# A decoder block on one core: the scores' place behind a pair's values, engine orders laid out anew, and four slices of a layer norm scaled on ScalarE

## The chip, the cores and the metric

One Trainium2 chip, of which the kernel uses one core. The metric is the device time of one execution in microseconds (us). A core has TensorE (matrix products, called PE in the profile), VectorE (DVE), ScalarE (ACT) and GpSimd (POOL), and SyncE (SP), whose instructions here are all DMA transfers. Each engine carries out its own list of instructions in order. The engines wait for one another by semaphores. TensorE writes into eight PSUM banks of 128 x 512 float32.

## The reference

Layer norm, cross attention with causal mask (32 query heads, 8 key and value heads), a gate and a residual; then layer norm, a gated feed-forward part with scaled weights, a gate and a residual. All in float32; x has 32 x 64 rows of 512.

```python
Q = (q @ Wq.T).reshape(b, s, HKV, exp, DK)      # q = layernorm(x), exp = 4, DK = 128
K = (k @ Wk.T).reshape(b, s, HKV, DK)           # k = v = ctx_4096
V = (v @ Wv.T).reshape(b, s, HKV, DV)
scores = jnp.einsum('bqhed,bkhd->bheqk', Q, K) * scale
scores = jnp.where(causal, scores, jnp.finfo(scores.dtype).min)
probs = jax.nn.softmax(scores, axis=-1)
attn = jnp.einsum('bheqk,bkhd->bqhed', probs, V).reshape(b, s, H * DV)
...
x = x + jnp.tanh(g_xattn[0]) * (attn @ Wd.T)
x = x + jnp.tanh(g_ffn[0]) * ffn(layernorm(x))  # silu(a) * b, then the down product
```

## The kernel before

Every large product is made of three products of rounded parts: a float32 operand is split into a high part (a rounded copy, made by ScalarE) and a low part (operand less high part, made by VectorE or GpSimd), and high x high, high x low and low x high are summed.

The program has three stages. In the first, 44 "quads" (0 to about 500 us) make values, keys and queries and write them to DRAM. The second is attention, from 500 to 985 us. The third is the feed-forward part, 28 blocks from 985 us to the end. The change is in the second stage and its borders.

Attention has NU = 64 units (a key head and 256 rows of x), which are taken in pairs: a step p of the loop `for p in range(2, NPAIR)` (NPAIR = 32) works with u = 2p. A unit passes through these functions, each on the engine named; "b" is one of two halves:

- `scores(u)` (PE): q times k into bank 6 (even u) or 7 (odd u).
- `turned(u)` (DVE): a transpose out of the bank into `prob`; `masked(u)` (POOL) adds the mask; `maxima(u)` (DVE) makes `own_max`; once per pair `other_maxima(p)` (ACT) moves the maxima across partitions, and `row_maxima(p)` (DVE) joins them.
- `less_max(u)` (POOL) subtracts, `exponentials(u)` (ACT), `sums(u)` (DVE) makes `own_sum`, `other_sums(p)` (ACT) moves, `inverse(p)` (DVE) makes `row_inv`, `over_sum(u)` (POOL) multiplies, `probs_turned(u)` (DVE) transposes into `pt`.
- `weighted_values(u)` (PE) makes pt times v into banks 4 and 5 (even u) or 2 and 3 (odd u); `out_hi(u)` (ACT) and `out_lo(u)` (DVE) split that into `o_hi[u % 2]` and `o_lo`.
- `output(i)`, i = 2u and 2u + 1 (PE): twelve matmuls with the split weights `wd_hi` and `wd_lo` into one bank; `add_to_x(i)` (DVE) multiplies by the gate and adds to X in SBUF.

The lines on which the order of these depends are waits on buffers. ScalarE's out_hi may overwrite o_hi only when the outputs of the unit two before are complete:

```python
        def out_hi(u):
            a.wait_ge(p_o, u + 1)
            if u >= 2:
                a.wait_ge(p_y, 2 * u - 2)
```

`p_y` counts outputs, `p_o` values, `v_y` additions to X, `v_turn` the transposes out of the score banks, `v_o` and `a_o` halves of out_lo and out_hi, `g_wd` low halves of wd. An output with t == 0 waits for out_lo of its unit and for its key head's four low halves of wd (`g_wd`, `output_lo` on POOL; the high halves, `output_hi`, on ACT); two of the four are made per step, the last two of head k in step 2k + 1. The outputs share banks 0 and 1, and every fourth one uses bank 6.

The second layer norm's slices 0 to 3 (two tiles of 128 rows each) are made ready inside the loop: in step 18 + 3m the statistics (`stats2`, `ln_moments` on DVE; `ln_pow`, and `apply2` for the scaling, on POOL), in the next step the transposes (`columns2` on PE) and their copies out of banks 2 and 3 (`x2_columns` on ACT, awaited by `weighted_values(u - 1)` through `a_xt2`) with `x2_sums` on POOL, and in the step after it the split (`x2_hi_of` on ACT, `x2_lo_of` on DVE, which waits for it). Step 30 holds POOL's and ACT's work for the first gate and up weights (`ffn_left_sums`, `ffn_left_lo`, `gate_up_hi`).

All orders are written out by hand, engine by engine.

## Time and profile before

| | |
|---|---|
| time, median of 3 runs | 1430.93 us (1430.73 to 1432.84) |
| the profiled execution: time, span | 1430.72 us, 1428.7 us |
| busy: PE, PEld, DVE | 1400.6, 1125.3, 1016.2 us |
| busy: ACT, POOL | 640.3, 1038.6 us |
| DMA traffic | 217.96 MB, mean 153 GB/s |

The span is what the profiler sees from the first to the last instruction; 2.0 us of the time lie outside it. PE is the matmul side of TensorE, PEld its loading of weights, which overlaps. An engine's busy time is what its instructions took, so its waits are the rest.

### The profile page before, as it was taken

The numbers are of one execution on the slowest core, as the hardware profiler recorded it, in microseconds if no ns is written. First come the engines' busy times: TensorE is split into PE (matmuls) and PEld (weight loads), VectorE is DVE, ScalarE is ACT, GpSimd is POOL, SyncE is SP. The second block draws the span as 40 slices with busy tenths as digits, with TensorE's granted clock in tenths as the row PEclk, the third lists the DMA queues.
The fourth block names the chain that finished last, engine by engine and source line by source line (L and its number), as shares of the span: only waits on it lengthen the run. The fifth ranks groups of instructions, "written<-read, shape, count | busy, mean of one in ns | idle before, by whom it ended". The sixth has DMA issues, their size and how long they took to land.

```text
span 1428.7 us, 19944 instructions
## 1 busy us (share of the span) xinstructions
PE 1400.6 (98%) x6810; PEld 1125.3 (79%) x6810; DVE 1016.2 (71%) x1549; ACT 640.3 (45%) x1246; POOL 1038.6 (73%) x919
## 2 busy tenths in 40 slices
PE   8999999999999999999999999999999999999998
PEld 8988788888887767777776766767888888888887
DVE  6487777777465677777776776775688878676776
ACT  6465555554444344443443444444344434343433
POOL 5599999998879556656656777775678886666664
PEclk9999999999999999999999999999999999999999
DMA  8477787778887745434443433331112112212112
GB/s 282 150 251 226 233 270 257 253 254 282 307 264 264 254 156 199 140 125 142 135 152 118 155 116 120 127 132 31 45 45 60 52 45 65 105 47 65 45 59 74
DMA packets 116067, 217.96 MB, mean 153 GB/s; under 512 B 9472, under 2 KB 47616, under 8 KB 113920
## 3 DMA queue, kind: packets, MB, share of 16 engines
q1 hardware_dynamic: 115968, 216.70, 46.1%
q8 instruction: 55, 0.90, 0.3%
q14 instruction: 44, 0.36, 0.1%
HBM read 151.13 MB, written 65.54 MB: 152 GB/s over the span
## 4 chain that ended last, share of the span: by engine, by line
PE 82%; POOL 8%; DVE 4%; issue 3%; ACT 1%; DMA 1%; SPq 0%; DVEq 0%; POOLq 0%; ACTq 0%
PE bank L574 65%; PE bank L848 3%; PE bank L849 3%; PE bank L850 3%; PE bank L697 3%; PE bank L722 3%; POOL prob L1663 2%; POOL xn L1677 1%; POOL wd_lo L1649 1%; POOL prob L1657 1%; POOL prob L1669 1%; DVE X L1386 1%; POOL wa_lo L1643 1%; PE bank L621 1%; DMA q_sb<-q_scratch 0%
## 5 line engine op out<-in xcount | busy, mean ns | idle before, releaser
L574 PE MATMUL bank<-xc,wa_hi 128*128 128x512 f32 x896 | 277.4, 391 | 0.0
L574 PE MATMUL bank<-wd_hi,o_hi 128*128 128x512 f32 x512 | 207.9, 406 | 5.0 <-issue 3.5
L574 PE MATMUL bank<-wd_lo,o_hi 128*128 128x512 f32 x512 | 200.8, 392 | 0.0
L574 PE MATMUL bank<-wd_hi,o_lo 128*128 128x512 f32 x512 | 199.5, 390 | 0.0
L574 PEld LDWEIGHTS bank<-xc,wa_hi 128*128 128x128 f32 x896 | 167.7, 188 | 36.4 <-issue 1.1
L574 PE MATMUL bank<-xc,wa_lo 128*128 128x512 f32 x448 | 174.5, 390 | 0.0
L1455 DVE SCALAR_TENSOR_TENSOR X<-bank,tg,X 128x512 f32<-128x512 f32 x221 | 154.5, 742 | 0.0
L574 PE MATMUL bank<-x_hi,wf_hi 128*128 128x512 f32 x392 | 153.0, 390 | 0.0
L574 PE MATMUL bank<-x_hi,wf_lo 128*128 128x512 f32 x392 | 152.6, 389 | 0.0
L574 PE MATMUL bank<-x_lo,wf_hi 128*128 128x512 f32 x364 | 141.7, 389 | 0.0
L1669 POOL TENSOR_TENSOR prob<-prob,row_inv 128x512 f32<-128x512 f32 x64 | 72.5, 1153 | 94.6 <-DVE row_inv L1356 94.6
L1386 DVE SCALAR_TENSOR_TENSOR X<-bank,tg,X 128x512 f32<-128x512 f32 x128 | 94.7, 741 | 65.2 <-PE bank L574 65.2
L574 PEld LDWEIGHTS bank<-wd_hi,o_hi 128*128 128x128 f32 x512 | 96.1, 188 | 47.9 <-issue 27.7
L574 PEld LDWEIGHTS bank<-wd_hi,o_lo 128*128 128x128 f32 x512 | 96.3, 188 | 21.3
L574 PEld LDWEIGHTS bank<-wd_lo,o_hi 128*128 128x128 f32 x512 | 96.3, 188 | 17.7
L1022 ACT ACTIVATE other_max<-own_max 32x32 f32<-32x32 f32 x128 | 29.1, 227 | 178.8 <-DVE own_max L1338 176.4
L1657 POOL TENSOR_TENSOR prob<-prob,mask 128x512 f32<-128x512 f32 x64 | 81.2, 1290 | 34.5 <-DVE prob L1334 34.5
L1300 DVE TENSOR_TENSOR t<-bank,s 128x512 f32<-128x512 f32 x44 | 30.3, 689 | 99.9 <-PE bank L574 99.7
L1375 DVE TENSOR_TENSOR o_lo<-bank,o_hi 128x512 fp32r<-128x512 f32 x128 | 82.1, 684 | 23.4 <-ACT o_hi L1042 23.4
L574 PEld LDWEIGHTS bank<-xc,wa_lo 128*128 128x128 f32 x448 | 84.1, 188 | 17.9
L1643 POOL TENSOR_TENSOR wa_lo<-w_raw,wa_hi 128x512 fp32r<-128x512 f32 x72 | 76.5, 1084 | 24.8 <-ACT wa_hi L951 24.7
L1643 POOL TENSOR_TENSOR wa_lo<-ws,wa_hi 128x1024 fp32r<-128x1024 f32 x36 | 92.5, 2570 | 0.0
(181 smaller groups left out, 3424.7 us busy)
## 6 DMA issues: line engine op xcount, KB each, us to landing
q_scratch<-q_st SPq DMA_DIRECT2D x32, 1024.0 KB, 4.4
q_sb<-q_scratch SPq DMA_DIRECT2D x64, 512.0 KB, 4.9
w_raw<-in_wq SPq DMA_DIRECT2D x32, 512.0 KB, 4.4
wd_raw<-in_wd SPq DMA_DIRECT2D x16, 1024.0 KB, 5.1
f_raw<-ffn_eff_scratch SPq DMA_DIRECT2D x28, 512.0 KB, 3.6
er_raw<-in_sf_r SPq DMA_DIRECT2D x42, 256.0 KB, 3.9
e_raw<-in_wf SPq DMA_DIRECT2D x42, 256.0 KB, 5.4
ffn_eff_scratch<-e_eff SPq DMA_DIRECT2D x42, 256.0 KB, 5.2
```

The costliest lines, as they stand in the source:

```text
L574: last = pe.matmul(to, a, b, start=(start and n == 0), stop=(stop and n == 3 * len(pairs) - 1), skip_group_check=onto)
L697: last = pe.matmul(bank[score_bank(u)][b * S:(b + 1) * S, t * 256:(t + 1) * 256], k_sb[u % 2][:, cb * S:(cb + 1) * S], q_sb[u % 2][:, :, c ...
L722: last = pe.matmul(bank[value_bank(u) + b][:, t * 256:(t + 1) * 256], v_sb[u % 2][rows, t, :], pt_of(u)[rows, t, :], start=True, stop=True)
L848: pe.matmul(to, d_hi[b][:, half, cols], dn_hi[n == NF - 1][:, :], start=True, stop=False)
L849: pe.matmul(to, d_hi[b][:, half, cols], dn_lo[n == NF - 1][:, :], start=False, stop=False)
L850: pe.matmul(to, d_lo[b][:, half, cols], dn_hi[n == NF - 1][:, :], start=False, stop=True).then_inc(p_yf, 1)
L1375: v.tensor_tensor(lo, bank[value_bank(u) + b][:, :].rearrange("p (t e s) -> p t e s", t=CT, e=G), f32(hi), ALU.subtract).then_inc(v_o, 1)
L1386: v.scalar_tensor_tensor(to, bank[output_bank(i)][:, :], tg[:, 0:1], to, ALU.mult, ALU.add).then_inc(v_y, 1)
L1455: v.scalar_tensor_tensor(to, bank[down_bank(n, k)][:, :], tg[:, 1:2], to, ALU.mult, ALU.add).then_inc(v_yf, 1)
L1643: g.tensor_tensor(wa_lo[p][:, part, :, :].rearrange("p n k d -> p (n k d)"), raw, f32(wa_hi[p][:, part, :, :]).rearrange("p n k d -> p (n ...
L1657: g.tensor_tensor(to, to, mask[:, :].rearrange("p (o k) -> p o k", o=1).broadcast_to([P, NR // 2, S]), ALU.add).then_inc(g_mask, 1)
L1669: g.tensor_tensor(to, to, row_inv[:, u % 2, :].rearrange("p (n o) -> p n o", o=1).broadcast_to([P, NR, HS]), ALU.mult).then_inc(g_p, 1)
```

## The change

The work is the same except for one thing: the scaling of slices 0 to 3 of the second layer norm, (x - mean) x rstd on GpSimd, becomes x x rstd + shift on ScalarE, with shift = -mean x rstd made by two small operations more. Everything else is order, and which bank an output uses (bank 6 goes from i % 4 == 3 to i % 4 == 1), so that waits on banks change with it.

On TensorE `scores(u + 2)` and `scores(u + 3)` stand directly behind the two `weighted_values`, where they stood two outputs later. SyncE loads q and k a pair earlier. On the other engines the step is written out anew. The core of the diff:

```diff
@@ PE: waits of scores and outputs
             if u >= 6 and u % 2 == 0:
-                pe.wait_ge(v_y, 2 * u - 8)
+                pe.wait_ge(v_y, 2 * u - 10)
...
-            elif i < 2 * NU - 4 and i % 4 == 3:
-
-                pe.wait_ge(v_turn, min(2 * ((i + 5) // 4), NU - 2) + 1)
+            elif i < 2 * NU - 4 and i % 4 == 1:
+
+                pe.wait_ge(v_turn, min((i + 7) // 2, NU - 2) + 1)
+            elif i == 2 * NU - 5:
+                pe.wait_ge(v_y, i - 1)
@@ PE: order
+        output(0)
         weighted_values(1)
-        output(0)
+        scores(4)
+        scores(5)
         for p in range(2, NPAIR):
             u = 2 * p
-            scores(u)
-            scores(u + 1)
             output(2 * u - 7)
...
             output(2 * u - 6)
             weighted_values(u - 2)
             weighted_values(u - 1)
+            if p + 1 < NPAIR:
+                scores(u + 2)
+                scores(u + 3)
             output(2 * u - 5)
             output(2 * u - 4)
@@ ACT
+        def apply2(m):
+            a.wait_ge(g_nm, 8 + m + 1)
+            if m:
+                a.wait_ge(p_xt2, 2 * m)
+            for p in range(2):
+                a.activation(xn2[:, p, :], X[:, 2 * m + p, :], ACT.Identity, bias=shift[:, p:p + 1],
+                             scale=rstd[:, p:p + 1]).then_inc(a_xn2, 1)
...
         for p in range(2, NPAIR):
             u = 2 * p
+            exponentials(u)
+            exponentials(u + 1)
+            other_sums(p)
             if p in WD_STEP:
                 k, heads = WD_STEP[p]
                 for e in heads:
                     output_hi(k, e)
             if p in COLUMNS1:
                 x2_columns(COLUMNS1[p], (2, 3))
-            other_maxima(p)
             out_hi(u - 2)
-            exponentials(u)
-            exponentials(u + 1)
+            out_hi(u - 1)
             if p in SPLIT1:
                 x2_hi_of(SPLIT1[p])
-            other_sums(p)
+            if p in ROWS1:
+                apply2(ROWS1[p])
+            if p + 1 < NPAIR:
+                other_maxima(p + 1)
             if p == F_FIRST:
                 for part in range(3):
                     gate_up_hi(0, part)
-            out_hi(u - 1)
@@ DVE: quad(NQ - 1), behind its second sum
+            if q == NQ - 1:
+                maxima(2)
+                maxima(3)
+                v.wait_ge(a_tanh, 1)
+                out_lo(0)
@@ DVE: the step
             add_to_x(2 * u - 8)
-            out_lo(u - 3)
-            turned(u)
-            turned(u + 1)
-            probs_turned(u - 2)
-            probs_turned(u - 1)
-            add_to_x(2 * u - 7)
-            maxima(u)
-            maxima(u + 1)
-            add_to_x(2 * u - 6)
-            row_maxima(p)
-            out_lo(u - 2)
             sums(u)
             sums(u + 1)
-            add_to_x(2 * u - 5)
+            add_to_x(2 * u - 7)
             inverse(p)
-            if p in SPLIT1:
-                x2_lo_of(SPLIT1[p])
             if p in ROWS1:
                 stats2(ROWS1[p])
                 ln_moments(8 + ROWS1[p])
+            if p in SPLIT1:
+                x2_lo_of(SPLIT1[p])
+            add_to_x(2 * u - 6)
+            out_lo(u - 2)
+            if p + 1 < NPAIR:
+                turned(u + 2)
+                turned(u + 3)
+            out_lo(u - 1)
+            probs_turned(u)
+            probs_turned(u + 1)
+            add_to_x(2 * u - 5)
+            if p + 1 < NPAIR:
+                maxima(u + 2)
+                maxima(u + 3)
+                row_maxima(p + 1)
@@ POOL: the step
-            over_sum(u - 2)
-            over_sum(u - 1)
-            masked(u)
-            masked(u + 1)
-            if p in COLUMNS1:
-                x2_sums(COLUMNS1[p])
+            over_sum(u)
+            over_sum(u + 1)
             if p in WD_STEP:
                 k, heads = WD_STEP[p]
                 for e in heads:
                     output_lo(k, e)
-            less_max(u)
-            less_max(u + 1)
             if p in ROWS1:
                 ln_pow(8 + ROWS1[p])
-                apply2(ROWS1[p])
+            if p + 1 < NPAIR:
+                masked(u + 2)
+                masked(u + 3)
+                less_max(u + 2)
+                less_max(u + 3)
+            if p in COLUMNS1:
+                x2_sums(COLUMNS1[p])
```

VectorE in step 20, the first split step, from `inverse(20)` on. Before (X_124 is X, o_lo1 with o_hi1 is unit 37, whose values are one step old, prob2 and prob3 are the buffers, in a ring of four, into which the next pair's scores are turned):

```order
L1356 RECIPROCAL row_inv_67<-row_sum_66 128x32
L1410 TENSOR_TENSOR x2_lo0_154<-xb2_151,x2_hi0_152 128x1792
L1386 SCALAR_TENSOR_TENSOR X_124<-bank1,tg_52,X_124 128x512
L1375 TENSOR_TENSOR o_lo1_147<-bank2,o_hi1_145 128x2x4x64
L1375 TENSOR_TENSOR o_lo1_147<-bank3,o_hi1_145 128x2x4x64
L1334 STREAM_TRANSPOSE prob2_136<-bank6 128x512
```

The same place after the change:

```order
L1386 RECIPROCAL row_inv_67<-row_sum_66 128x32
L1443 TENSOR_TENSOR x2_lo0_154<-xb2_151,x2_hi0_152 128x1792
L1416 SCALAR_TENSOR_TENSOR X_124<-bank1,tg_52,X_124 128x512
L1405 TENSOR_TENSOR o_lo0_146<-bank4,o_hi0_144 128x2x4x64
L1405 TENSOR_TENSOR o_lo0_146<-bank5,o_hi0_144 128x2x4x64
L1364 STREAM_TRANSPOSE prob2_136<-bank6 128x512
L1364 STREAM_TRANSPOSE prob3_137<-bank7 128x512
L1405 TENSOR_TENSOR o_lo1_147<-bank2,o_hi1_145 128x2x4x64
```

The low part x2_lo0 stands behind the reciprocal both times; what follows it is now out_lo of both units of this step's values, with the transposes between them.

ScalarE in step 20. Before:

```order
L1022 ACTIVATE other_max_62<-own_max_61 32x32 x4
L1042 ACTIVATE o_hi0_144<-bank4 128x2x4x64
L1042 ACTIVATE o_hi0_144<-bank5 128x2x4x64
L1035 ACTIVATE prob0_134<-prob0_134 128x512
L1035 ACTIVATE prob1_135<-prob1_135 128x512
L1068 ACTIVATE x2_hi0_152<-xb2_151 128x1792
L1030 ACTIVATE other_sum_65<-own_sum_64 32x32 x4
L1042 ACTIVATE o_hi1_145<-bank2 128x2x4x64
```

After:

```order
L1043 ACTIVATE other_sum_65<-own_sum_64 32x32 x4
L1028 ACTIVATE wd_hi0_126<-wd_raw_125 128x512 x2
L1055 ACTIVATE o_hi0_144<-bank4 128x2x4x64
L1055 ACTIVATE o_hi0_144<-bank5 128x2x4x64
L1055 ACTIVATE o_hi1_145<-bank2 128x2x4x64
L1055 ACTIVATE o_hi1_145<-bank3 128x2x4x64
L1089 ACTIVATE x2_hi0_152<-xb2_151 128x1792
L1035 ACTIVATE other_max_62<-own_max_61 32x32 x4
```

The high part x2_hi0, for which VectorE's x2_lo0 waits, has moved from ahead of the moved sums and of o_hi1 to behind both.

GpSimd where steps 30 and 31 meet (fs and wf are the first gate and up weights). Before:

```order
L1649 TENSOR_TENSOR wd_lo1_129<-wd_raw_125,wd_hi1_127 128x512 x2
L1663 TENSOR_TENSOR prob0_134<-prob0_134,row_max_63 128x512
L1663 TENSOR_TENSOR prob1_135<-prob1_135,row_max_63 128x512
L1699 TENSOR_TENSOR fs_160<-f_raw_159 128x256
...
L1710 TENSOR_TENSOR wf_lo_158<-fs_160,wf_hi_157 128x1024
L1669 TENSOR_TENSOR prob0_134<-prob0_134,row_inv_67 128x512
L1669 TENSOR_TENSOR prob1_135<-prob1_135,row_inv_67 128x512
L1657 TENSOR_TENSOR prob2_136<-prob2_136,mask_51 128x512
L1657 TENSOR_TENSOR prob3_137<-prob3_137,mask_51 128x512
L1649 TENSOR_TENSOR wd_lo1_129<-wd_raw_125,wd_hi1_127 128x512 x2
L1663 TENSOR_TENSOR prob2_136<-prob2_136,row_max_63 128x512
```

After:

```order
L1701 TENSOR_TENSOR prob2_136<-prob2_136,row_max_63 128x512
L1701 TENSOR_TENSOR prob3_137<-prob3_137,row_max_63 128x512
L1737 TENSOR_TENSOR fs_160<-f_raw_159 128x256
...
L1748 TENSOR_TENSOR wf_lo_158<-fs_160,wf_hi_157 128x1024
L1707 TENSOR_TENSOR prob2_136<-prob2_136,row_inv_67 128x512
L1707 TENSOR_TENSOR prob3_137<-prob3_137,row_inv_67 128x512
L1687 TENSOR_TENSOR wd_lo1_129<-wd_raw_125,wd_hi1_127 128x512 x2
```

The last two low halves of wd stood ahead of the last pair's subtraction of the maxima (prob2, prob3 with row_max); now they stand behind it, behind the weights' seven operations and behind that pair's multiplication with row_inv.

## Rows read from the trace of the kernel before

**Rows 1.** The page's busy time of one engine: us, share of span, instructions

```profile
PE 1400.6 (98%) x6810; PEld 1125.3 (79%) x6810; DVE 1016.2 (71%) x1549; ACT 640.3 (45%) x1246; POOL 1038.6 (73%) x919
```

**Rows 2.** Timeline of a plain step: start us, length us, engine, line, out<-in [idle before <-releaser]

```profile
673.76 1.95 PE L697 MATMUL bank<-q_sb,k_sb 128*64 128x256 f32 x16
...
675.63 0.50 PE L574 MATMUL bank<-wd_hi,o_hi 128*128 128x512 f32 x1
...
675.97 0.40 PE L574 MATMUL bank<-wd_lo,o_hi 128*128 128x512 f32 x1
...
678.69 0.75 DVE L1386 SCALAR_TENSOR_TENSOR X<-bank,tg,X 128x512 f32<-128x512 f32 x1 [0.47 <-PE bank L574]
...
681.30 2.00 PE L722 MATMUL bank<-pt,v_sb 64*128 64x256 f32 x16
...
682.48 1.09 ACT L1042 ACTIVATE o_hi<-bank 128x512 fp32r<-128x512 f32 x2 [0.84 <-PE bank L722]
683.18 1.29 DVE L1375 TENSOR_TENSOR o_lo<-bank,o_hi 128x512 fp32r<-128x512 f32 x2 [0.92 <-ACT o_hi L1042]
...
683.22 0.50 PE L574 MATMUL bank<-wd_hi,o_hi 128*128 128x512 f32 x1
```

**Rows 3.** Timeline of the entry into the loop, 503 to 515 us

```profile
504.26 0.19 DVE L1344 TENSOR_TENSOR row_max<-own_max,other_max 128x32 f32<-128x32 f32 x1 [1.05 <-ACT other_max L1022]
...
504.53 2.06 POOL L1663 TENSOR_TENSOR prob<-prob,row_max 128x512 f32<-128x512 f32 x2 [7.67 <-DVE row_max L1344]
...
508.00 0.98 ACT L1030 ACTIVATE other_sum<-own_sum 32x32 f32<-32x32 f32 x4 [0.75 <-DVE own_sum L1348]
...
509.67 2.05 POOL L1669 TENSOR_TENSOR prob<-prob,row_inv 128x512 f32<-128x512 f32 x2 [3.09 <-DVE row_inv L1356]
...
514.39 2.00 PE L722 MATMUL bank<-pt,v_sb 64*128 64x256 f32 x16
```

**Rows 4.** Timeline of the stop behind slice 1's columns, 833 to 837 us

```profile
833.31 0.98 ACT L1030 ACTIVATE other_sum<-own_sum 32x32 f32<-32x32 f32 x4 [0.75 <-DVE own_sum L1348]
...
834.08 3.07 PE L697 MATMUL bank<-q_sb,k_sb 128*64 128x256 f32 x16 [2.75 <-DVE X L1386]
```

**Rows 5.** Timeline of the end of the loop, 960 to 975 us

```profile
961.67 0.74 POOL L1699 TENSOR_TENSOR fs<-f_raw 128x256 f32<-128x256 f32 x1
...
969.14 2.06 POOL L1669 TENSOR_TENSOR prob<-prob,row_inv 128x512 f32<-128x512 f32 x2
...
973.43 2.00 PE L722 MATMUL bank<-pt,v_sb 64*128 64x256 f32 x16
```

**Rows 6.** Timeline of VectorE's hand-overs without a wait, 785 to 792 us

```profile
785.44 1.28 DVE L1375 TENSOR_TENSOR o_lo<-bank,o_hi 128x512 fp32r<-128x512 f32 x2
...
786.64 1.30 DVE L1334 STREAM_TRANSPOSE prob<-bank 128x512 f32<-128x512 f32 x2
...
787.87 1.26 DVE L1362 STREAM_TRANSPOSE pt<-prob 128x512 f32<-128x512 f32 x2
789.09 0.75 DVE L1386 SCALAR_TENSOR_TENSOR X<-bank,tg,X 128x512 f32<-128x512 f32 x1
789.76 1.27 DVE L1338 TENSOR_REDUCE own_max<-prob 128x16 f32<-128x512 f32 x2
...
791.06 0.98 ACT L1022 ACTIVATE other_max<-own_max 32x32 f32<-32x32 f32 x4 [4.43 <-DVE own_max L1338]
```

**Rows 7.** Timelines of POOL, ACT and DVE around slice 0, 755 to 801 us

```profile
765.93 4.14 POOL L1677 TENSOR_SCALAR xn<-X,moments,rstd 128x512 f32<-128x512 f32 x2
...
777.42 2.51 POOL L1649 TENSOR_TENSOR wd_lo<-wd_raw,wd_hi 128x512 fp32r<-128x512 f32 x2
...
795.37 1.69 ACT L1068 ACTIVATE x_hi<-xb 128x1792 fp32r<-128x1792 f32 x1
...
798.59 1.96 DVE L1410 TENSOR_TENSOR x_lo<-xb,x_hi 128x1792 fp32r<-128x1792 f32 x1
```

**Rows 8.** Busy time and granted TensorE clock (PEclk) of one stretch

```profile
834.60:838.00 3.40, 3.40 (x16) 2.12 (x13) 3.40 (x7) 1.95 (x4) 2.68 (x3) 0.52 0.40 150
```

More of the change, by code:

```diff
@@ L203, in flamingo @@
     a_c0, a_chi, a_k, a_w1, a_tanh = sem("a_c0"), sem("a_chi"), sem("a_k"), sem("a_w1"), sem("a_tanh")
+    a_xn2 = sem("a_xn2")
     a_xt, a_xhi, a_wa, a_s1, a_s5, a_c11 = (sem("a_xt"), sem("a_xhi"), sem("a_wa"), sem("a_s1"), sem("a_s5"),
@@ L290, in flamingo @@
     NPAIR = NU // 2
+    SHARED = (0, None, 1, 2)
     def output_bank(i):
@@ L294, in output_bank @@
             return 4 + i - (2 * NU - 4)
-        return 6 if i % 4 == 3 else (3 * (i // 4) + i % 4) % 2
+        return 6 if i % 4 == 1 or i == 2 * NU - 5 else (3 * (i // 4) + SHARED[i % 4]) % 2
     def output_before(i):
-        n = 3 * (i // 4) + i % 4 - 2
-        return 4 * (n // 3) + n % 3
+        n = 3 * (i // 4) + SHARED[i % 4] - 2
+        return 4 * (n // 3) + SHARED.index(n % 3)
     def score_bank(u):
@@ L500, in _ @@
                 load_v(3)
+                load_q_k(6)
+                load_q_k(7)
             if q == Q0 + NHP:
@@ L532, in _ @@
             u = 2 * p
-            for n in range(u + 2, min(u + 4, NU)):
-                load_q_k(n)
             load_v(u)
             load_v(u + 1)
+            for n in range(u + 4, min(u + 6, NU)):
+                load_q_k(n)
             if p == 4:
@@ L735, in output @@
                 pe.wait_ge(a_c11, NQ)
-            elif i == 1:
+            elif i == 2:
                 pe.wait_ge(v_t2, NQ)
-            elif i < 2 * NU - 4 and i % 4 == 3:
-                pe.wait_ge(v_turn, min(2 * ((i + 5) // 4), NU - 2) + 1)
+            elif i < 2 * NU - 4 and i % 4 == 1:
+                pe.wait_ge(v_turn, min((i + 7) // 2, NU - 2) + 1)
+            elif i == 2 * NU - 5:
+                pe.wait_ge(v_y, i - 1)
             elif i < 2 * NU - 4:
@@ L748, in columns2 @@
             for p in range(2):
-                pe.wait_ge(g_xn, 2 * m + p + 1)
+                if m < 4:
+                    pe.wait_ge(a_xn2, 2 * m + p + 1)
+                else:
+                    pe.wait_ge(g_xn, 2 * (m - 4) + p + 1)
                 for k in range(KC):
@@ L1181, in _ @@
         other_maxima(1)
+        out_hi(1)
         exponentials(2)
@@ L1184, in _ @@
         other_sums(1)
-        out_hi(1)
+        other_maxima(2)
         for p in range(2, NPAIR):
             u = 2 * p
+            exponentials(u)
+            exponentials(u + 1)
+            other_sums(p)
             if p in WD_STEP:
@@ L1242, in ln_moments @@
             v.wait_ge(v_bn, 2 * n + 2)
-            if 1 <= n <= 8:
+            if 1 <= n <= 12:
                 v.wait_ge(g_nm, n)
@@ L1248, in ln_moments @@
             v.tensor_scalar(veps[:, :], moments[:, :, 1], EPS, None, ALU.add).then_inc(v_eps, 1)
-            if n < 8:
+            if n < 12:
                 v.tensor_scalar(neg_mean[:, :], moments[:, :, 0], -1.0, None, ALU.mult).then_inc(v_nm, 1)
@@ L1390, in stats2 @@
             if m:
-                v.wait_ge(g_xn, 2 * m)
+                if m <= 4:
+                    v.wait_ge(a_xn2, 2 * m)
+                else:
+                    v.wait_ge(g_xn, 2 * (m - 4))
             ln_bn(lambda p: X[:, 2 * m + p, :])
@@ L1479, in _ @@
             quad(q)
-        v.wait_ge(a_tanh, 1)
-        out_lo(0)
-        maxima(2)
-        maxima(3)
         row_maxima(1)
+        out_lo(1)
         sums(2)
         sums(3)
+        turned(4)
+        turned(5)
         inverse(1)
+        probs_turned(2)
+        probs_turned(3)
+        maxima(4)
+        maxima(5)
+        row_maxima(2)
         for p in range(2, NPAIR):
@@ L1510, in _ @@
                 ln_moments(8 + ROWS1[p])
+            if p in SPLIT1:
[13 more added lines that the diff above has]
+                row_maxima(p + 1)
         add_to_x(2 * NU - 8)
-        out_lo(NU - 3)
-        probs_turned(NU - 2)
-        probs_turned(NU - 1)
         for i in range(2 * NU - 7, 2 * NU - 4):
@@ L1599, in ln_pow @@
                 g.wait_ge(a_xn, 2 * n)
+            elif 8 < n <= 12:
+                g.wait_ge(a_xn2, 2 * (n - 8))
             g.tensor_tensor(rstd[:, :], veps[:, :], neg_half[:, :], ALU.pow).then_inc(g_pow, 1)
-            if n < 8:
+            if n < 12:
                 g.wait_ge(g_pow, n + 1)
@@ L1787, in _ @@
         less_max(3)
+        over_sum(2)
+        over_sum(3)
+        masked(4)
+        masked(5)
+        less_max(4)
+        less_max(5)
         for p in range(2, NPAIR):
             u = 2 * p
-            over_sum(u - 2)
-            over_sum(u - 1)
-            masked(u)
-            masked(u + 1)
-            if p in COLUMNS1:
-                x2_sums(COLUMNS1[p])
+            over_sum(u)
+            over_sum(u + 1)
             if p in WD_STEP:
@@ L1808, in _ @@
                     ffn_left_lo(0, part)
-        over_sum(NU - 2)
-        over_sum(NU - 1)
         for n in range(NF):
```

## The prediction

> **What bounds the kernel now.** I read the engines' busy table first: TensorE is busy for 98% of the span [rows 1], so only a stop of TensorE, or a change in what it executes, can move the time. Then I read the timeline of the stretch in which attention's pairs run, 505 to 980 us, because every edit lies there. In what follows a step p is one turn of the pair loop (u = 2p), V is the start of its pair of values on TensorE and Sc the start of its pair of scores. From V of step 2 at 514.39 to a plain V at 681.30 there are 11 steps [rows 2, 3], so a plain step takes 166.91 / 11 = 15.17 us. In it TensorE never stops: scores go from 673.76 to 675.63 (1.87), values from 681.30 to 683.22 (1.92), and the remaining 11.38 are four outputs, 2.85 each [rows 2]. VectorE and GpSimd trail behind in that step, and their order costs nothing. It does cost at the four slices of the second layer norm, where TensorE stops, for example 2.75 us ahead of the scores at 834.08, until VectorE's addition to X has emptied bank 6 [rows 4]. All of step 2 to step 31 is 973.43 - 514.39 = 459.04 us [rows 3, 5]; 29 plain steps are 439.9, so the four slices cost 19.1 us, some 4 of them the transposes themselves (32 of 128 columns, an estimate from the 512-column matmuls' 0.23), 15 stops.
>
> **What the joining of values and scores gives.** The first output matmul after scores is followed by the next after 0.34 us (675.63 to 675.97), where an output's twelve average 2.85 / 12 = 0.24 [rows 2]: changing from one kind of matmul to another costs about 0.1 going out, and I take as much going in. Scores directly behind values save the way out of one block and the way in of the next, about 0.2 per step (from 0 to 0.4). TensorE alone would then need 15.17 - 0.2 = 14.97 us a step. The 30 joinings are worth 6 us (0 to 12), provided that nothing else becomes slower than 14.97.
>
> **The plain step afterwards.** I follow what has to happen between one Sc and the next. ScalarE now stands with out_hi(u-1) right behind out_hi(u-2), and VectorE has out_lo(u-1), probs_turned, add_to_x(2u-5) and maxima(u+2) behind one another. But out_hi(u-1) overwrites the half of o_hi that output(2u-5) reads (its wait on p_y is 2u-4), and output(2u-5) stands behind the scores. So from Sc: 1.87 scores and 3.06 until the other engines see that output complete (675.63 to 678.69) [rows 2] make 4.93; o_hi to o_lo 0.70 (682.48 to 683.18) [rows 2]; o_lo 1.20, the turned probabilities 1.22, one addition 0.67, two maxima until ScalarE moves them 1.30, by the starts 785.44, 786.64, 787.87, 789.09, 789.76, 791.06 [rows 6]; the move 0.98 and 0.03 of hand-over [rows 6]; row_max to less_max 0.27 and less_max to other_sum 3.47 [rows 3]; other_sum to the released scores 0.77 (833.31 to 834.08), which holds add_to_x(2u-3) of bank 6 [rows 4]. The sum is 15.54. These are one loop: add_to_x(2u-3) must be done for scores(u+4). It is 0.57 longer than TensorE's 14.97 and 0.37 longer than the step now. In the order of before nothing closes this loop, since out_hi(u-1) stands behind the sums and is not waited for by the maxima.
>
> In odd steps GpSimd's low halves of wd are needed by output(2u-4). They start 2.02 behind over_sum, which starts 3.47 + 1.67 behind less_max (508.00 to 509.67) [rows 3], take 2.51 [rows 7], and 0.2 of hand-over follows: 9.9 from less_max, and less_max of this pair lies at Sc - 4.24. So output(2u-4) starts at Sc + 5.65 in place of 1.87 + 2.87 = Sc + 4.74; of these 0.9 us the slack of 0.57 swallows the larger part, 0.34 is left. Plain steps: 15.54 even, 15.88 odd.
>
> **The entry.** The first output now waits for out_lo(0) about as long as values(1) waited. Then over_sum(2) starts near 510.0 (509.67 now) [rows 3], with masked(4), (5) behind it: 2.02 + 2.5 (as wd_lo, the row of GpSimd that is nearest) [rows 7], the last maximum 0.7, its move 1.01, 0.27: less_max(4) at 516.6. scores(6) need add_to_x(1), so Sc of step 2 is 516.6 + 4.24 = 520.8, while values(3) end at about 516.5: a stop of 4.3 us. From Sc of step 2 to Sc of step 18 there are 16 plain steps: 8 x 15.54 + 8 x 15.88 = 251.4, that is 772.2.
>
> **The slices, three steps each.** (a) The step with the statistics, and on to the next Sc: x2_columns stand on ScalarE behind other_sums and two copies, and values(u-1) wait for them. less_max at Sc + 11.30 (15.54 - 4.24); then 3.47 + 0.98, two copies 1.1 and two more 1.1 (as the o_hi pair, 1.09 [rows 2]), hand-overs 0.3: 18.3; half the values 1.0: the next Sc at +19.3. (b) The step with the columns: 15.54. (c) The step with the split: x2_lo_of stands on VectorE ahead of add_to_x(2u-6), out_lo(u-2) and both turned, but x2_hi_of stands on ScalarE behind out_hi(u-1), which waits for output(2u-5). So Sc + 4.93, o_hi 1.06, x_hi 1.69, x_lo from 7.72 until 9.60 (1.96 less overlap) [rows 7], the addition 0.67, out_lo 1.28, hand-over 0.15: output(2u-4), wanted at 4.74, starts at 11.7, a stop of 7.0 us. Going on with turned 1.20 behind out_lo's start at 10.25, then 1.22 to out_lo(u-1) at 12.67, 1.20, 1.22, 0.67, 1.30, 1.01, 0.27 gives less_max at 18.3 and the next Sc at 22.6. The three make 57.4 in place of 3 x 15.17 + 4.8 = 50.3. Four slices: 229.6, so Sc of step 30 is 1001.8.
>
> **The way out.** In step 31 output(120) needs the last low halves of wd. They stood ahead of less_max(62); now they stand behind it, behind the seven GpSimd operations for the first gate and up weights (961.67 to 969.14, 7.47) [rows 5] and behind over_sum(62). less_max(62) at 1001.8 + 11.3 = 1013.1; 2.03 + 7.47, or by way of ScalarE, whose exponentials now wait behind the copy of those weights, 9.7; then 2.02 + 2.51 + 0.2: output(120) at 1027.6, after a stop of 8 us. Now it starts at 973.43 + 1.92 + 2.87 = 978.2 [rows 5]. Everything behind it (the last outputs, the feed-forward part) is unchanged and its inputs are early, so it shifts by 1027.6 - 978.2 = 49.4 us.
>
> **The clock.** After the stop that ends at 834.08 the granted clock was 0.52 for 3.4 us, the level of 1.2 GHz, and that pair of scores took 3.07 in place of 1.95 [rows 2, 4, 8]; such a dip costs 3.4 x 0.5 = 1.7 us on TensorE. I count it once for the entry, once for the way out, and for the four split steps 1.1 each (their 0.6 of slack covers a part): 7.8 us. The sum: 1430.7 (the profiled execution, 0.2 under the median of the runs) + 49.4 + 7.8 = 1488 us.
>
> **Moving the scaling of slices 0 to 3.** GpSimd loses 4.14 us per slice [rows 7]; ScalarE gains two activations, costed at nothing: they stand between out_hi(u-1), done at Sc + 6.0, and other_maxima, which can't start before Sc + 10.0. If that cover were gone, each would add its own time, some 0.7. The Trainium skill (GPSIMD Engine Reference, Engine selection) says that an elementwise operation with one input runs on GpSimd at roughly line rate. By that the move would free only about 1.5 us per slice; the trace has 2.07 for each of the two [rows 7], and the trace decides. The sum would be the same by either, since GpSimd is not in the loop of a plain step.
>
> **The rivals.** *Faster:* the longer way from scores to values (eight outputs in place of six) covers everything. TensorE goes at 14.97, and with 4 x 4.14 us taken from GpSimd the stops at the slices vanish: 1430.7 - 6 - 15 = 1410. It holds if the loop above is under 14.97 and x2_hi_of doesn't wait for an output. For it: GpSimd's waits and scaling are what the slices wait on now. Against it: 15.54 by rows, and the order itself. *The split does not stop TensorE:* say it finds its high half early; 4 x 7.0 and four dips less: 1455. *The loop does not bind plain steps:* hand-overs overlap better; 16 steps at about 14.97 in place of 15.71: 12 us less, and 2 at the slices: 1474. *All stops dip the clock,* the 3.3 us ones at the columns too (now the one of [rows 4] dipped, and no other): four more at 1.7, and 0.6 at each split: 1497. *It evens out:* the joinings pay for one stop: 1431.
>
> **How the numbers follow.** Forecast 0.70 (its own range 1474 to 1499, from 0 to 12 for the joinings, 0.2 either way in 27 loops, and dips from none to all); 1497 and beyond 0.05; split harmless 0.09; loop not binding 0.08; faster 0.06; even 0.02. To leave out no more than 2 in 10 the range reaches down to the harmless split: 1455 to 1500. A measurement tells about 0.2% (3 us) from no change. Faster 0.06, the same 0.02, slower 0.92.
>
> **What would show it.** In the profile after: plain steps of 15.5 to 15.9 us from V to V, with a stop of about half a microsecond ahead of scores, waiting for VectorE's addition; o_hi of the second unit right behind the third output after the values; a stop of about 4 us ahead of scores(6); four of about 7 ahead of output(2u-4) while VectorE waits for x_hi; about 3 inside the values of the columns steps; about 8 in step 31 behind wd_lo. I am wrong if plain steps run at 15.0, or if x_lo doesn't hold VectorE up.

## The result, and the profile after

The changed kernel takes 1495.78 us (median of 4 runs, 1494.75 to 1495.96), the kernel before 1431.88 on the same chip. The ratio of the two means is 1.0443 (95% interval 1.0425 to 1.0461), so it is 4.4% slower. The forecast was 1488 in a range of 1455 to 1500. The profiled execution took 1495.64 us, its span is 1493.8.

The page's busy line of the changed kernel, against [rows 1]:

```profile
PE 1412.2 (95%) x6810; PEld 1138.1 (76%) x6810; DVE 1017.3 (68%) x1553; ACT 641.5 (43%) x1254; POOL 1015.3 (68%) x915
```

TensorE executes the same 6810 matmuls, 11.6 us longer (they run at half the clock behind stops), and it is idle in 5% of the span in place of 2%. What it waited for from 520 to 1050 us, in the view of waits (us in total, times, longest):

```profile
PE bank L579 <- DVE o_lo L1405: 27.1, 4, 6.8
PE bank L727 <- ACT xb L1074: 12.8, 4, 3.2
PE bank L702 <- DVE X L1416: 9.8, 13, 2.6
PE bank L579 <- POOL wd_lo L1687: 7.8, 1, 7.8
PE bank L579 <- ACT o_hi L1055: 6.2, 8, 0.9
```

The first line is the four split steps (outputs wait for out_lo), the second the four steps with columns (values wait for x2_columns), the third the even plain steps and the four columns steps (scores wait for an addition to X) with the entry, the fourth step 31, the fifth the eight odd plain steps.

Three pairs of scores follow one another in plain steps, from TensorE's timeline:

```profile
555.19 1.95 PE L702 MATMUL bank<-q_sb,k_sb 128*64 128x256 f32 x16
...
570.77 1.95 PE L702 MATMUL bank<-q_sb,k_sb 128*64 128x256 f32 x16 [0.60 <-DVE X L1416]
...
586.68 1.95 PE L702 MATMUL bank<-q_sb,k_sb 128*64 128x256 f32 x16
```

15.58 and 15.91 us, where [rows 2] gave 15.17. The stop of the odd step, ahead of output(2u - 4):

```profile
573.69 2.52 POOL L1687 TENSOR_TENSOR wd_lo<-wd_raw,wd_hi 128x512 fp32r<-128x512 f32 x2
...
576.42 0.47 PE L579 MATMUL bank<-wd_hi,o_hi 128*128 128x512 f32 x1 [0.76 <-ACT o_hi L1055]
```

The view names ScalarE's o_hi, but the one made just then is unit u - 1's, and by its code this output waits for unit u - 2's, made 3 us earlier. Of all that it does wait for, GpSimd's wd_lo ends last.

The split step of slice 0, all engines:

```profile
815.62 1.08 ACT L1055 ACTIVATE o_hi<-bank 128x512 fp32r<-128x512 f32 x2 [2.65 <-PE bank L579]
816.60 1.70 ACT L1089 ACTIVATE x_hi<-xb 128x1792 fp32r<-128x1792 f32 x1
818.33 2.02 DVE L1443 TENSOR_TENSOR x_lo<-xb,x_hi 128x1792 fp32r<-128x1792 f32 x1 [6.59 <-ACT x_hi L1089]
820.27 0.74 DVE L1416 SCALAR_TENSOR_TENSOR X<-bank,tg,X 128x512 f32<-128x512 f32 x1
820.93 1.28 DVE L1405 TENSOR_TENSOR o_lo<-bank,o_hi 128x512 fp32r<-128x512 f32 x2
...
822.31 0.77 PE L579 MATMUL bank<-wd_hi,o_hi 128*128 128x512 f32 x1 [6.78 <-DVE o_lo L1405]
```

Read it downwards: ScalarE's o_hi of the second unit waits for an output; x_hi stands behind it; VectorE has waited 6.59 us for x_hi, and the addition and o_lo stand behind x_lo. The first matmul takes 0.77, since the clock has fallen. Here are busy times, with the granted clock after the engines, of the 4.2 us behind that stop and of the stretch behind the columns stop of slice 1:

```profile
822.30:826.50 4.20, 4.19 (x10) 3.33 (x11) 4.20 (x8) 0.00 (x0) 2.52 (x2) 0.50 0.00 0
...
852.60:857.30 4.70, 4.66 (x25) 2.49 (x25) 2.01 (x3) 0.87 (x2) 3.77 (x4) 0.64 0.22 51
```

The four stops of 6.8 us and the one of 7.8 were all followed by the level of 1.2 GHz; of the four of 3.2 us, two were (slices 1 and 3), two were not. The way out, GpSimd and ScalarE, and the output that waits:

```profile
1031.18 1.06 ACT L1108 ACTIVATE wf_hi<-fs 128x1024 fp32r<-128x1024 f32 x1 [4.29 <-POOL fs L1742]
1032.14 1.13 ACT L1048 ACTIVATE prob<-prob 128x512 f32<-128x512 f32 x2
...
1035.92 2.05 POOL L1707 TENSOR_TENSOR prob<-prob,row_inv 128x512 f32<-128x512 f32 x2 [0.51 <-DVE row_inv L1386]
...
1037.93 2.50 POOL L1687 TENSOR_TENSOR wd_lo<-wd_raw,wd_hi 128x512 fp32r<-128x512 f32 x2
1040.64 0.77 PE L579 MATMUL bank<-wd_hi,o_hi 128*128 128x512 f32 x1 [7.79 <-POOL wd_lo L1687]
```

So the account of the profiled executions is, by the start of output(120) and of the scores: 1040.64 against 978.2, 62.4 us later; 2.1 us more by the last pair's values (the clock behind that stop), 0.6 to the end: 65.1.

### The profile page after: what moved, and what is told of

Same layout as the page of the kernel before. It is cut to its first block, busy times and chain, and to the rows that moved or that the text cites. A ratio compares the mean times of both kernels' runs of the same rounds, so it can differ in the third digit from the quotient of the medians.

```text
span 1493.8 us, 19964 instructions
## 1 busy us (share of the span) xinstructions
PE 1412.2 (95%) x6810; PEld 1138.1 (76%) x6810; DVE 1017.3 (68%) x1553; ACT 641.5 (43%) x1254; POOL 1015.3 (68%) x915
## 4 chain that ended last, share of the span: by engine, by line
PE 73%; DVE 10%; POOL 6%; ACT 5%; issue 4%; DMA 2%; SPq 1%; DVEq 0%; ACTq 0%; POOLq 0%
PE bank L579 56%; PE bank L702 4%; PE bank L862 3%; PE bank L863 3%; PE bank L861 3%; POOL prob L1701 3%; PE bank L727 2%; DVE o_lo L1405 2%; DVE X L1416 2%; DVE own_max L1368 1%; ACT o_hi L1055 1%; ACT other_max L1035 1%; DVE pt L1392 1%; DVE own_sum L1378 1%; DMA er_raw<-in_sf_r 1%
## 5 line engine op out<-in xcount | busy, mean ns | idle before, releaser
L579 PE MATMUL bank<-wd_lo,o_hi 128*128 128x512 f32 x512 | 204.2, 399 | 0.0
L579 PE MATMUL bank<-wd_hi,o_lo 128*128 128x512 f32 x512 | 204.2, 399 | 0.0
L579 PEld LDWEIGHTS bank<-wd_hi,o_hi 128*128 128x128 f32 x512 | 99.2, 194 | 82.5 <-issue 50.9
L1701 POOL TENSOR_TENSOR prob<-prob,row_max 128x512 f32<-128x512 f32 x64 | 65.9, 1051 | 128.4 <-DVE row_max L1374 128.4
L1707 POOL TENSOR_TENSOR prob<-prob,row_inv 128x512 f32<-128x512 f32 x64 | 65.8, 1048 | 92.7 <-DVE row_inv L1386 92.7
L1055 ACT ACTIVATE o_hi<-bank 128x512 fp32r<-128x512 f32 x128 | 68.8, 591 | 106.2 <-PE bank L579 99.5
L579 PEld LDWEIGHTS bank<-wd_lo,o_hi 128*128 128x128 f32 x512 | 99.4, 194 | 19.6
```

The lines of the kernel that those rows point to most:

```text
L579: last = pe.matmul(to, a, b, start=(start and n == 0), stop=(stop and n == 3 * len(pairs) - 1), skip_group_check=onto)
L1055: a.activation(o_hi[u % 2][:, :, :].rearrange("p e (t b s) -> p b t e s", t=CT, b=2)[:, b], bank[value_bank(u) + b][:, :].rearrange("p (t ...
L1701: g.tensor_tensor(to, to, row_max[:, u % 2, :].rearrange("p (n o) -> p n o", o=1).broadcast_to([P, NR, HS]), ALU.subtract).then_inc(g_sub, 1)
L1707: g.tensor_tensor(to, to, row_inv[:, u % 2, :].rearrange("p (n o) -> p n o", o=1).broadcast_to([P, NR, HS]), ALU.mult).then_inc(g_p, 1)
```

## The experiments

Eleven kernels ran, all measured against the kernel before on their own chip, whose medians were 1432.1 to 1432.6. "Changed" below is the changed kernel.

**Split step.** VectorE's low half at the end of the step.

```diff
-            if p in SPLIT1:
-                x2_lo_of(SPLIT1[p])
             add_to_x(2 * u - 6)
...
                 row_maxima(p + 1)
+            if p in SPLIT1:
+                x2_lo_of(SPLIT1[p])
```

> The changed kernel with one edit: VectorE's x2_lo_of of the split steps moved to the end of the step, behind row_maxima(p + 1). My theory (VectorE waits for ScalarE's x2_hi_of, which stands behind out_hi(u - 1), and out_lo(u - 2) stands behind it): all four stops of 6.8 us ahead of output(2u - 4) and their clock dips go, a split step falls from 23.9 or 24.4 us between scores to 15.6 or 15.9, the kernel from 1496 to about 1463. Rival (what stops TensorE there is the addition or out_hi itself, and the low half only rides along): the stops stay above 4 us and the time above 1485.

Measured: 1470.44 us (1468.13 to 1473.31), ratio 1.0266 (1.0249 to 1.0282), 25 us under changed. The waits for o_lo are gone altogether, so the mechanism holds. But it is 7 us above what I expected: split steps take 17.3 to 17.6 us where I had put 15.6 or 15.9. The timeline shows why:

```profile
822.12 2.02 DVE L1443 TENSOR_TENSOR x_lo<-xb,x_hi 128x1792 fp32r<-128x1792 f32 x1
...
822.28 3.77 POOL L1701 TENSOR_TENSOR prob<-prob,row_max 128x512 f32<-128x512 f32 x2 [3.08 <-DVE row_max L1374]
```

GpSimd's pair of less_max takes 3.77 us there and 2.06 in every other step. I tested that by doing the operation twice, with the same values.

```diff
                 if blk == 0:
+                    v.tensor_tensor(to[:, s]..., xb2[:, ...]..., x2_hi[...]..., ALU.subtract).then_inc(v_twice, 1)
+                    v.wait_ge(v_twice, m + 1)
```

> The kernel with x2_lo_of at the end of the split step, whose time was 7 us above what I expected, with that operation done twice in a row, the same values both times. My theory (GpSimd's less_max starts 0.16 us behind it and makes no headway while VectorE works on x2_lo, so that the pair takes 3.77 in place of 2.06 us): the pair then takes 5.5 to 5.8, the four steps get 2 us longer each, about 1478 (1475 to 1483). Rival (the 3.77 comes from something else, and VectorE has 3 us idle there that hide a second operation): less_max stays at 3.77 and the time within 3 us of 1470.

Measured: 1481.69 us (1480.19 to 1484.57), 11 above the single one. GpSimd's pair, and VectorE's second subtraction, now take:

```profile
822.43 5.55 POOL L1708 TENSOR_TENSOR prob<-prob,row_max 128x512 f32<-128x512 f32 x2 [3.06 <-DVE row_max L1375]
...
824.32 2.75 DVE L1450 TENSOR_TENSOR x_lo<-xb,x_hi 128x1792 fp32r<-128x1792 f32 x1
```

The theory holds: GpSimd makes next to no headway while VectorE works on x_lo. It goes the other way too: the second subtraction takes 2.75 us where the first takes 2.02, with GpSimd's first operation of the pair between the two. The time is in the range that I gave, though the median rose by 11 us where I had put 8: in the profiled executions (9.5 us apart) the four split steps are 1.4 to 1.8 us longer each, the three steps behind them 0.5 to 1.3, and one columns step 1.6, by a further clock dip.

**Plain step.** The cut of the loop, and of one other term of it.

```diff
-            out_lo(u - 1)
             probs_turned(u)
             probs_turned(u + 1)
             add_to_x(2 * u - 5)
             if p + 1 < NPAIR:
                 maxima(u + 2)
                 maxima(u + 3)
+            out_lo(u - 1)
+            if p + 1 < NPAIR:
                 row_maxima(p + 1)
```

> The changed kernel with one edit: VectorE's out_lo(u - 1) moved behind probs_turned, add_to_x(2u - 5) and the two maxima, so that the maxima of the next pair no longer wait for an output that stands behind the scores. My theory (a loop of 15.5 to 15.9 us from scores to scores by way of output(2u - 5), out_hi(u - 1), out_lo(u - 1), maxima, sums, add_to_x): plain steps fall to TensorE's own 14.9 to 15.0, the stops ahead of scores and in odd steps behind wd_lo go, the columns stops shrink from 3.2 to about 1, and the time falls from 1496 to about 1468; the split stops of 6.8 us stay. Rival (the plain step is bound by GpSimd's or the scores' own hand-overs): plain steps stay at 15.5 or more and the time above 1490.

Measured: 1460.90 us (1459.86 to 1464.11), ratio 1.0202 (1.0187 to 1.0217): 35 us under changed, 7 better than expected. Every plain step is TensorE's own:

```profile
552.85 1.95 PE L702 MATMUL bank<-q_sb,k_sb 128*64 128x256 f32 x16
...
567.76 1.95 PE L702 MATMUL bank<-q_sb,k_sb 128*64 128x256 f32 x16
...
582.68 1.95 PE L702 MATMUL bank<-q_sb,k_sb 128*64 128x256 f32 x16
```

The waits that are left, 520 to 1060 us:

```profile
PE bank L579 <- DVE o_lo L1405: 31.9, 5, 6.8
PE bank L702 <- DVE X L1416: 4.3, 1, 4.3
PE bank L727 <- ACT xb L1074: 3.1, 4, 1.0
```

Thirteen waits for the addition have become one (the entry), the waits for o_hi are gone, the columns stops fell from 3.2 to 1.0 without a clock dip. In step 31 the wait for wd_lo shrank to one of 4.8 us for o_lo.

The second cut leaves out_lo(u - 1) where the change put it and takes the turned probabilities out from behind it:

```diff
             out_lo(u - 1)
-            probs_turned(u)
-            probs_turned(u + 1)
             add_to_x(2 * u - 5)
             if p + 1 < NPAIR:
                 maxima(u + 2)
                 maxima(u + 3)
+            probs_turned(u)
+            probs_turned(u + 1)
+            if p + 1 < NPAIR:
                 row_maxima(p + 1)
```

> The changed kernel with one edit: VectorE's probs_turned(u), (u + 1) (1.2 us) moved out from between out_lo(u - 1) and the maxima, to behind them; out_lo(u - 1) stays where the change put it. It asks whether the loop is a sum of terms, as my prediction had it, so that taking out any term of it shortens the step by that term until TensorE's own 14.91 is reached. By the loop: even plain steps fall from 15.58 by up to 1.2, that is to 14.91; odd ones keep 0.1 to 0.4 of stop behind the low halves of wd; the columns and split stops shrink by 1.2 each: 1472 us (1468 to 1480). Rival (only the wait for output(2u - 5) itself matters, what stands between is hidden): plain steps stay at 15.6 and 15.9, above 1490.

Measured: 1479.39 us (1477.29 to 1482.60), ratio 1.0326 (1.0308 to 1.0344). Plain steps are 14.91 and 15.49 us; outside the entry the wait for the addition is gone, and the four columns stops are 8.3 us together, from 12.8. So the loop is a sum, as forecast. That the split stops would shrink by 1.2 us too was wrong: they are 6.8 still, since the turned probabilities stand behind out_lo(u - 2) there and are no part of that stop; this is 5 of the 7 us by which I missed.

**Way out.** The last halves of the output weights in step 30, ahead of less_max(62).

```diff
@@ ACT, step 30, ahead of other_maxima(p + 1), and no longer in step 31
+            if p == NPAIR - 2:
+                for e in WD_STEP[NPAIR - 1][1]:
+                    output_hi(WD_STEP[NPAIR - 1][0], e)
@@ POOL, step 30, ahead of less_max(u + 2), and no longer in step 31
+            if p == NPAIR - 2:
+                for e in WD_STEP[NPAIR - 1][1]:
+                    output_lo(WD_STEP[NPAIR - 1][0], e)
```

> The changed kernel with one edit: the last two halves of the output weights (high on ScalarE, low on GpSimd) made one step earlier, in step 30 ahead of less_max(62) and of the first gate and up weights. My theory (output(120) waits for them behind seven operations and over_sum(62)): the stop of 7.8 us in step 31 and its clock dip go, 1496 to about 1487, all else unchanged. Rival (over_sum(62), turned or the values of the last pair are as late, and the stop only moves behind output(120)): above 1493.

Measured: 1492.65 us (1491.63 to 1494.49), ratio 1.0421 (1.0405 to 1.0437). That is 6 us above what I expected and just under what the rival had (above 1493). Neither was quite right: the stop neither went nor moved behind output(120), but stayed ahead of it, went from 7.8 to 4.9 us and changed its name.

```profile
1030.56 1.06 ACT L1108 ACTIVATE wf_hi<-fs 128x1024 fp32r<-128x1024 f32 x1 [4.30 <-POOL fs L1745]
1031.53 1.13 ACT L1048 ACTIVATE prob<-prob 128x512 f32<-128x512 f32 x2
1033.48 0.98 ACT L1043 ACTIVATE other_sum<-own_sum 32x32 f32<-32x32 f32 x4 [0.83 <-DVE own_sum L1381]
1034.49 2.06 ACT L1055 ACTIVATE o_hi<-bank 128x512 fp32r<-128x512 f32 x4
...
1037.09 0.77 PE L579 MATMUL bank<-wd_hi,o_hi 128*128 128x512 f32 x1 [4.86 <-DVE o_lo L1408]
```

ScalarE waits 4.3 us for GpSimd's sums of the first gate and up weights; exponentials(62), the sums and o_hi queue behind that copy. So I moved those weights too:

```diff
@@ ACT and POOL: in step 30
-            if p == F_FIRST:
-                ...
@@ ACT and POOL: behind the loop
+        for part in range(3):
+            gate_up_hi(0, part)
...
+        ffn_left_sums(0)
+        for part in range(3):
+            ffn_left_lo(0, part)
```

> The changed kernel with the last halves of the output weights a step earlier, as before, and now also the first gate and up weights, GpSimd's and ScalarE's, behind the loop. In the run with the weights alone a stop of 4.9 us stayed in step 31: out_lo waited for ScalarE, whose exponentials(62) stood behind the copy of the gate and up weights. My theory (these two are the whole way-out loss): no stop in step 31 and no clock dip behind it, 1496 to 1486 (1484 to 1488). Rival (a third wait, of the feed-forward weights that are now late or of the last values): 1490 or more.

Measured: 1489.67 us (1486.05 to 1491.55), ratio 1.0395 (1.0368 to 1.0423). No stop is left in step 31, and from its values to the last pair's it takes 19.1 us in place of 28.6: 9.4 less, near the 10 that I expected. The median gained 6 us only, and lies above the range that I gave (1484 to 1488). In its profiled run 2.3 us are lost between values(1) and values(4): there a clock dip falls on scores(6) and what follows, where TensorE is the bound, while in the changed kernel's profile it fell ahead of a stop that would have come anyway.

**Scaling.** Put back on GpSimd in the changed kernel, behind less_max(u + 3) of the same step.

```diff
@@ ACT
-            if p in ROWS1:
-                apply2(ROWS1[p])
@@ POOL
                 less_max(u + 3)
+            if p in ROWS1:
+                apply2(ROWS1[p])
```

> The changed kernel with the scaling of slices 0 to 3 put back on GpSimd, behind less_max as before. By my prediction's words (GpSimd is not in the loop, the sum is the same by either): 1496, no change. By the trace of the joining alone: the scaled rows come at 17.5 us after the scores, and the transposes want them at 10.5; about 4 to 5.5 us per slice are added, 1508 to 1520. What it tells apart is whether the scaling's move hid a part of what the new orders cost.

Measured: 1515.68 us (1514.98 to 1516.64), ratio 1.0577 (1.0562 to 1.0592): 20 us slower than changed.

```profile
789.85 4.14 POOL L1705 TENSOR_SCALAR xn<-X,moments,rstd 128x512 f32<-128x512 f32 x2
...
792.08 0.72 PE L758 MATMUL bank<-ident_r,xn_cols 128*128 128x128 f32 x4 [5.22 <-POOL xn L1705]
...
794.05 0.75 PE L758 MATMUL bank<-ident_r,xn_cols 128*128 128x128 f32 x4 [1.25 <-POOL xn L1705]
```

TensorE's transposes wait for each of the two. And the reverse, the kernel before with the scaling on ScalarE alone, by the changed kernel's apply2:

```diff
@@ ACT
             out_hi(u - 1)
+            if p in ROWS1:
+                apply2(ROWS1[p])
@@ POOL
                 ln_pow(8 + ROWS1[p])
-                apply2(ROWS1[p])
```

> The kernel before with the scaling alone: slices 0 to 3 scaled on ScalarE (behind out_hi(u - 1), shift made by the two small operations), all orders as before. My theory now (in the slices' steps TensorE's transposes wait for GpSimd's 4.15 us of scaling, and the multiplications by row_inv behind it are late too): most of the 15 us of stops goes, 1432 to about 1418. Rival (the scaling is not on the path, the cost at nothing that my prediction gave it, and the stops belong to the copies and VectorE): within 4 us of the kernel before.

Measured: 1417.67 us (1416.94 to 1418.00), ratio 0.9894 (0.9881 to 0.9907). In the slices' stretch TensorE has no wait at all in the view of waits; in the kernel before it had 12.0 us there from 755 to 980 (7.5 for the addition to X, 1.0 for the scaled rows, 3.5 that the view gives to no releaser).

**Joining.** The kernel before, with the scores behind the values, the changed banks and loads, and `turned` between sums and add_to_x(2u - 5).

```diff
@@ PE
             weighted_values(u - 1)
+            if p + 1 < NPAIR:
+                scores(u + 2)
+                scores(u + 3)
             output(2 * u - 5)
@@ DVE
-            turned(u)
-            turned(u + 1)
...
             sums(u + 1)
+            if p + 1 < NPAIR:
+                turned(u + 2)
+                turned(u + 3)
             add_to_x(2 * u - 5)
```

> The kernel before with the joining alone: scores(u + 2), (u + 3) directly behind the values, the banks and the loads of q and k as in the changed kernel, VectorE's turned of that pair placed behind sums; every other order and the scaling on GpSimd as before. My theory (the joining itself saves 0.26 us a step, as the steps of 14.91 in the changed kernel's trace show, and the loss comes from the orders around it): plain steps of 14.91, and some of the 15 us of stops at the slices gone too since the addition that scores wait for is an older one: about 1419 us (1410 to 1424). Rival (scores behind values press the chain from scores to values or the banks, whatever the other orders): a stop in each step and no less than 1431.

Measured: 1427.52 us (1426.93 to 1428.70), ratio 0.9966 (0.9952 to 0.9981). The plain steps are 14.91 as expected, but the time is above my range (1410 to 1424): the slices' stops stayed, under other names (waits of TensorE, 755 to 980 us):

```profile
PE bank L756 <- POOL xn L1688: 8.2, 8, 1.5
PE bank L578 <- DVE prob L1342: 2.0, 2, 1.1
PE bank L578 <- issue: 1.8, 5, 0.5
```

All eight scaled tiles are late. With both the joining and the scaling on ScalarE:

> The kernel before with the joining and the scaling on ScalarE, and nothing of the other orders. My theory: both gains add up, plain steps of 14.91 and slices with little stop: about 1412 (1407 to 1419), so that the change without its new orders of VectorE, ScalarE and GpSimd would have been faster than before by over 1%. Rival (the slices' stops are the price of the joining or of VectorE's and ScalarE's copies): 1423 or more.

Measured: 1413.70 us (1412.84 to 1415.44), ratio 0.9868 (0.9856 to 0.9881), 1.3% under the kernel before and the fastest of all. Its busy line:

```profile
PE 1395.9 (99%) x6810; PEld 1127.2 (80%) x6810; DVE 1012.1 (72%) x1553; ACT 644.8 (46%) x1254; POOL 1022.2 (72%) x915
```

**All mended.** Four edits from above together in the changed kernel: x2_lo_of last, out_lo(u - 1) behind the maxima, and both on the way out.

> The changed kernel with four things undone or moved at once: out_lo(u - 1) behind the maxima, x2_lo_of at the end of the split step, the last two halves of the output weights a step earlier, and the first gate and up weights (GpSimd and ScalarE) behind the loop. My theory (these three waits are all of the loss beside the entry): plain steps of 14.91, split steps under 16, no stop in step 31, about 1420 (1414 to 1428), under the kernel before. Rival (the stops are taken over by others, as behind wd_early, or the joining's order has a loss of its own): over 1435.

Measured: 1426.30 us (1423.87 to 1431.98), ratio 0.9959 (0.9943 to 0.9975), 69 us under changed. TensorE's waits from 520 to 1050 us:

```profile
PE bank L727 <- ACT xb L1074: 6.4, 4, 2.1
PE bank L702 <- DVE X L1418: 4.3, 1, 4.3
PE bank L579 <- ACT o_hi L1055: 1.5, 2, 0.8
```

It is still 12.6 us behind joined_act. Between the two profiled executions (each the slowest of its kernel, 16.5 us apart) 5.7 us lie in the entry (the stop of 4.3 and the clock behind it) and 10.6 in the steps of the slices, 6.4 of these in waits for the copies of the columns, which stand behind the sums on ScalarE.

## Why the prediction was right, and where it was not

**The joining.** I took 0.2 us a step (0 to 0.4); it is 15.17 - 14.91 = 0.26. In whole kernels it gave 4.0 us (joined_act against before_act) and 4.9 (joined_alone), not 6, as the slices' steps take some of it back.

**The plain step.** The loop was forecast at 15.54 and 15.88 us, and the steps are 15.58 and 15.91, with the two stops where it put them: output(2u - 4) of the odd step starts 5.65 us behind the scores (570.77 to 576.42), as forecast by way of wd_lo. That it is this loop is shown by both cuts: without out_lo(u - 1) in it the steps are 14.91, without the turned probabilities 14.91 and 15.49. The rival in which the loop does not bind is out, and with the four stops of 6.8 us so is the one in which the split does no harm.

**The entry.** A stop of 4.3 us ahead of scores(6) was forecast, with the scores at 520.8, 25.8 us behind the first values (494.98 before). They came 25.7 us behind them, at 523.67: the first values themselves were 3.0 us late. That need not be the change's doing: in the changed kernel and the eight made from it they start between 494.9 and 499.6, though the code is the same up to there. The stop is 2.6 us in this profile and 4.3 in seven of those eight, because here the clock was 0.60 from 511.8 to 515.2 and stretched the outputs ahead of it. The dip of 1.7 us that I had added behind the stop did not come here, and the one that came cost nothing.

**The slices.** The step with statistics: 19.3 forecast, 19.15 measured. Columns: 15.54, measured 15.60 (slices 0 and 2) and 17.27 (1 and 3, a clock dip that I had given only to the rival in which all stops dip). Split: a stop of 7.0 forecast, 6.78 measured, and 22.6 plus 1.1 us for the clock forecast, 23.9 and 24.4 measured. Three steps cost 58.7 and 60.8 in place of 57.4 + 1.1. The twelve took 239.0 us where I had 234.0, the largest single miss, and it is the size of the clock term: the dips behind the splits lasted 4.2 to 5.4 us where I had taken 3.4, and two of the columns dips were left out.

**The way out.** From Sc of step 30 to output(120) I forecast 25.8 us; it is 25.76, the stop 7.8 for "about 8". Of the two ways that I worked out there, the one through ScalarE was no footnote, though: taking away the wait for wd_lo alone left 4.9 us.

**The sum.** 1488 was 7.6 us short of the profiled execution: 2.0 before the slices (3.0 in the first stage, 0.8 in sixteen plain steps, less 0.1 in the entry and the dip of 1.7 that cost nothing), 5.0 in them, and the rest behind step 31. These are terms that were mis-sized; no mechanism among them failed. One figure ahead of the sum was not what its working gives: 32 transposes at a quarter of 0.23 us are 1.8 us, not "some 4". Measured in before_act, whose slices have no stop, a slice is 0.87 us longer than three plain steps, 3.5 us for the four. The figure is no term of the 1488.

**The scaling.** Here a step failed, though the time did not show it. I wrote that the sum would be the same with the scaling on either engine, since GpSimd is not in the loop of a plain step. It is 20 us dearer on GpSimd in the changed kernel (pool_scale), and on ScalarE it alone makes the kernel before 15 us faster (before_act). A slice's step is no plain step: 4.14 us of GpSimd [rows 7] stand between the statistics and TensorE's transposes, and ahead of the next pair's multiplications and masks. I had read the stop of [rows 4] by its releaser, the addition to X, and gave it to VectorE; the addition was late because of what stood ahead on GpSimd. The trace of the kernel before shows it, followed back from that stop:

```profile
815.85 4.14 POOL L1677 TENSOR_SCALAR xn<-X,moments,rstd 128x512 f32<-128x512 f32 x2
...
829.85 2.05 POOL L1663 TENSOR_TENSOR prob<-prob,row_max 128x512 f32<-128x512 f32 x2
...
831.59 0.69 DVE L1348 TENSOR_REDUCE own_sum<-prob 128x16 f32<-128x512 f32 x1 [3.35 <-ACT prob L1035]
...
833.20 0.74 DVE L1386 SCALAR_TENSOR_TENSOR X<-bank,tg,X 128x512 f32<-128x512 f32 x1
```

From 815.85 to 831.90 GpSimd has no idle time: the scaling, over_sum, the masks, x2_sums, wd_lo and less_max follow one another. ScalarE's exponentials wait for less_max, VectorE's sums for the exponentials, and the addition stands behind the sums. In before_act the waits for the addition go with the scaling. The two activations cost ScalarE 1.52 us a pair, near the estimate (0.7 each), and nothing on the path. On the rule of the Trainium skill (GPSIMD Engine Reference, Engine selection), that a one-input operation runs at roughly line rate on GpSimd, the runs side with the trace and not with the 1.5 us that I took by it: the pair is 4.14 us again in pool_scale.

Taken apart, then: scaling on ScalarE -15 us, joining -4, and the new orders of VectorE, ScalarE and GpSimd about +82 (1495.8 against 1413.7), with whatever the parts do to one another.

## What to carry to other kernels

When a block of work is put ahead of another on the engine that is the bound, list for every wait of the other engines whether it now needs something that stands behind the block, and add up the way round: a loop of 15.5 us under a cover of 15.2 costs only 0.4 a step, but it takes away all the slack, so that every late thing then stops the engine in full. When an engine waits for two others in a row (a low half for a high half), look up what each of them stands behind and what stands behind it: here the low half could be moved to the end of the step, and the stop went with it. A releaser's name is the last link, not the cause: ask what stood ahead of it on its own engine before an operation is costed at nothing.

## What the runs showed that I had not expected

VectorE's subtraction of x_lo (128 x 1792, both operands in SBUF) holds GpSimd up: the pair of GpSimd operations that starts 0.16 us behind it takes 3.77 us in place of 2.06, in four of four steps of xlo_last and of mended, and 5.55 with the subtraction done twice. In the changed kernel nothing of GpSimd ran beside it. The Trainium skill (SBUF — State Buffer, SBUF: two separate sides) says that the two engines share a pair of ports as an exclusive lock, and that a VectorE instruction with two SBUF inputs, if it starts first, keeps it for its whole length against a GpSimd instruction that reads SBUF. These runs agree with that. 1.71 us more in each of four steps is 6.8 us, about what xlo_last missed by.

The same stop does not always dip the clock: 3.2 us at the columns were followed by 1.2 GHz in slices 1 and 3, and not in 0 and 2. And a dip costs nothing when it lies ahead of a stop that waits for others, as in the changed kernel's entry; an experiment that moves it shows some 2 us that are not its edit's (way_out above).
